# First rows re-laid in a graph-network kernel: norms ahead of unit rows, masks ahead of conversions

## The reference

```python
h = jnp.maximum(_layernorm(x, axis=-1), 0.0)
x = x + _L0_gnn_ref(h, adj, L0_gnn_beta)   # cosine attention, masked by adj
h = jnp.maximum(_layernorm(x, axis=-1), 0.0)
x = x + _L1_gnn_ref(h, adj, W_self, W_neigh)  # h @ W_self + (adj @ h / deg) @ W_neigh
# _L0_gnn_ref:
norm2 = jnp.linalg.norm(x, axis=1, keepdims=True)
cos = beta[0] * (x @ x.T) / (norm2 @ norm2.T + 1e-07)
P = jax.nn.softmax(cos + (1.0 - adj) * -1000000000.0, axis=1)
return P @ x
```

## Time and profile before

| | |
|---|---|
| three runs | 503.0 us median (502.96 to 504.5) |
| profiled execution | 502.87 us, span 500.9 us |
| busy share of the span | TensorE 94%, GpSimd 59%, ScalarE 60%, VectorE 56% |
| chain of waits | TensorE 87%, VectorE 5%, GpSimd 3%, DMA 2%, ScalarE 2% |

### The profile page before, as it was taken

How to read it: one execution, slowest core, us unless ns; L and a number is a source line. 1 busy time by engine, 2 the same in 40 slices (tenths; PEclk the granted TensorE clock), 3 DMA queues, 4 the chain that set the end, 5 groups by cost and what they waited for, 6 DMA issues and landing times.

```text
span 500.9 us, 12746 instructions
## 1 busy us (share of the span) xinstructions
PE 471.2 (94%) x5392; PEld 397.7 (79%) x5392; DVE 279.8 (56%) x686; ACT 298.1 (60%) x427; POOL 297.0 (59%) x261
## 2 busy tenths in 40 slices
PE   0768999999999999999999999999799999999996
PEld 0636788888788888888888888877688888888895
DVE  6975666567566585656765856757632321322153
ACT  2979787866986759876798598688730201110121
POOL 3889887877897768986799688888750000000000
PEclk9989999999999999999999999999999999999999
DMA  8057865655776557754676476563010000000001
GB/s 248 12 183 282 273 204 175 224 178 183 252 249 221 181 161 249 245 217 157 225 244 236 167 227 223 205 196 107 3 34 1 22 22 22 1 22 22 22 1 43
DMA packets 31549, 74.39 MB, mean 149 GB/s; under 512 B 2560, under 2 KB 15104, under 8 KB 31488
## 3 DMA queue, kind: packets, MB, share of 16 engines
q1 hardware_dynamic: 31488, 73.54, 43.8%
HBM read 71.43 MB, written 2.10 MB: 147 GB/s over the span
## 4 chain that ended last, share of the span: by engine, by line
PE 87%; DVE 5%; POOL 3%; DMA 2%; ACT 2%; issue 1%; SPq 0%; POOLq 0%; DVEq 0%; ACTq 0%
PE ps L1078 23%; PE ps L941 17%; PE ps L952 9%; PE ps L1005 6%; PE ps L1002 6%; PE ps L1004 6%; PE ps L979 5%; PE ps L982 5%; PE ps L981 5%; PE ps L1063 2%; PE ps L1052 2%; DVE adj_t L665 1%; DVE adj_t L644 1%; DMA stage<-in_adj_dram 1%; DMA x_sb<-in_x_dram 1%
## 5 line engine op out<-in xcount | busy, mean ns | idle before, releaser
L407 POOL TENSOR_TENSOR near<-word,adj_t 128x1024 f32<-128x1024 f32 x72 | 145.2, 2016 | 57.4 <-DVE word L778 56.4
L561 ACT ACTIVATE word<-ps,small 128x512 f16<-128x512 f32 x144 | 135.6, 942 | 70.8 <-PE ps L941 67.0
L778 DVE TENSOR_TENSOR word<-ps,word 128x512 f16<-128x512 f32 x144 | 106.3, 739 | 105.4 <-ACT ps L562 105.3
L1078 PE MATMUL ps<-table,adj_t 128*128 128x257 f16 x1024 | 116.8, 274 | 0.0
L941 PE MATMUL ps<-unit_t 128*128 128x512 f16 x432 | 106.7, 381 | 4.7 <-DVE word L778 4.7
L1078 PEld LDWEIGHTS ps<-table,adj_t 128*128 128x128 fp8e4 x1024 | 99.3, 98 | 13.0
L562 ACT ACTIVATE ps<-ps,small 128x512 f32<-128x512 f32 x144 | 107.2, 744 | 0.0
L1002 PE MATMUL ps<-table,near 128*128 128x129 f16 x576 | 102.6, 219 | 4.0 <-POOL near L407 2.6
L1005 PE MATMUL ps<-table,near 128*128 128x129 f16 x576 | 102.8, 222 | 0.0
L1004 PE MATMUL ps<-table,near 128*128 128x128 f16 x576 | 102.6, 219 | 0.0
L979 PE MATMUL ps<-table,far 128*128 128x129 f16 x448 | 79.9, 219 | 0.3
(11 more groups left out here) (94 smaller groups left out, 490.6 us busy)
## 6 DMA issues: line engine op xcount, KB each, us to landing
stage<-in_adj_dram SPq DMA_DIRECT2D x128, 512.0 KB, 4.4
x_sb<-in_x_dram SPq DMA_DIRECT2D x4, 512.0 KB, 6.2
x_again<-in_x_dram SPq DMA_DIRECT2D x8, 256.0 KB, 5.6
out_dram<-x_sb SPq DMA_DIRECT2D x7, 256.0 KB, 2.3
out_dram<-x_sb SPq DMA_DIRECT2D x1, 192.0 KB, 2.0
stage<-in_L_gnn_W_neigh_dram SPq DMA_DIRECT2D x1, 64.0 KB, 2.6
stage<-in_L_gnn_W_self_dram SPq DMA_DIRECT2D x1, 64.0 KB, 2.5
out_dram<-x_sb SPq DMA_DIRECT2D x1, 64.0 KB, 1.7
```

What stands on the lines that cost most here:

```text
L407: pool.tensor_tensor(ring(near, k), ring(word, k), adj_t[:, near_adj(k)], ALU.mult).then_inc(s_near, 1)
L561: act.activation(half(word16, k, c, 0, HIGH, TPS), score(k, c), ACT.Exp, bias=exp_bias, scale=exp_scale)
L778: dve.tensor_tensor(half(word16, k, c, 0, LOW, TPS), score(k, c), half(word16, k, c, 0, HIGH, TPS), ALU.subtract).then_inc(s_elo, 1)
L1078: return pe.matmul(ps[:, agg_bank(g) + t, 0:TW], adj_t[:, at:at + P], tab(b), start=(b == 0), stop=(b == T - 1))
```

## The change

The head's order is rewritten, and with it the first iterations of the middle. VectorE takes all four parts' statistics before the first norms, and all norms before its unit rows. The scale by HS = 256 is folded into small operations on GpSimd ahead of its powers; two small VectorE operations per part go. GpSimd takes all four powers of the variances ahead of the first norm power; its conversions of pair 2 stand behind mask 0. ScalarE does table_high(0) and units(3) behind its h tiles. The low half of the table of block 0 goes to VectorE. units(4) to units(6) go into VectorE's iterations 1, 3 and 5, units(7) into GpSimd's 6 and 7. TensorE sums all h tiles before the first scores; its order up to iteration 1 changes, and the first three transposes use other PSUM banks. SyncE loads two near and two far tiles at once. ScalarE converts its far tiles one pair later.

The diff, cut to its core:

```diff
-    RING = [("unit", 0), ("unit", 1), ("score", 0, 0), ("score", 0, 1), ("score", 1, 0), ("score", 1, 1), ("unit", 2)]
+    RING = [("score", 0, 0), ("score", 0, 1), ("score", 1, 0), ("score", 1, 1)]
...
-    LEAD = 3
+    CONVERT_AFTER = [[2], [3], [4], [5], [6, 7]] + [[k + 3] if k + 3 < NP else [] for k in range(5, NP)]
...
-            return 5 + AT["unit", g] % 3
+            return (3, 4, 2)[g] if g < 3 else 5 + AT["unit", g] % 3
...
+            load_near(0)
+            load_near(1)
+            load_far(FAR[0])
+            load_far(FAR[1])
+            for k in range(2, NP):
+                sp.wait_ge(s_adjd, k - 1)
+                load_near(k)
+                m = FAR_BEFORE[k]
+                if PAIR[k][2] and m >= 2:
+                    sp.wait_ge(far_sem(m), m // 2)
+                    load_far(k)
...
-                                   ).then_inc(s_rnorm_s, 1)
+                pool.tensor_scalar(var_e[:, part], mv_v[:, part, 1], HS ** -2, EPS * HS ** -2, ALU.mult, ALU.add
+                                   ).then_inc(s_scaled_e, 1)
+                pool.wait_ge(s_scaled_e, i + 1)
+                pool.tensor_tensor(scale_h[:, part], var_e[:, part], neg_half, ALU.pow).then_inc(s_rstd, 1)
+
+            def inverse_norms(first, last):
+
+                part = slice(first * TX, (last + 1) * TX)
+                pool.wait_ge(s_norm2, last + 1)
+                pool.tensor_scalar(norm2_g[:, part], norm2[:, part], HS ** -2, 1e-20 * HS ** -2, ALU.mult, ALU.max
+                                   ).then_inc(s_scaled_n, 1)
+                pool.wait_ge(s_scaled_n, min(last, 2) + 1)
+                for i in range(first, last + 1):
+                    part = slice(i * TX, (i + 1) * TX)
+                    pool.tensor_tensor(rnorm[:, part], norm2_g[:, part], neg_half, ALU.pow).then_inc(s_rnorm, 1)
...
-                for t in range(g * TPS, (g + 1) * TPS):
-                    pool.tensor_scalar(u_rows(t, t + 1), h_rows(t, t + 1), rnorm[:, t:t + 1], HS, ALU.mult, ALU.mult
-                                       ).then_inc(s_unit_p, 1)
+                for t in range(g * TPS + a, g * TPS + b):
+                    pool.tensor_scalar(u_rows(t, t + 1), h_rows(t, t + 1), rnorm[:, t:t + 1], None, ALU.mult).then_inc(s_unit_p, 1)
...
-            inverse_norm(0)
+            inverse_std(3)
+            inverse_norms(0, 0)
             units(0)
-            inverse_std(3)
-            inverse_norm(1)
-            scaled_inverse_norm(1)
             convert(0)
-            inverse_norm(2)
+            inverse_norms(1, 1)
...
-            inverse_norm(3)
-            units(7)
+            inverse_norms(2, 3)
             convert(1)
-            convert(2)
-            convert_far(2)
...
-                if s == 0 and k % 2 == 0:
-                    low_parts(k // 2)
-                if k + LEAD < NP:
-                    convert(k + LEAD)
-                    if PAIR[k + LEAD][2] and FAR_BEFORE[k + LEAD] % 2 == 0:
-                        convert_far(k + LEAD)
+                if s == 0 and k % 2 == 1 and (k + 1) // 2 < NS:
+                    low_parts((k + 1) // 2)
+                for ahead in CONVERT_AFTER[k]:
+                    convert(ahead)
+                    if PAIR[ahead][2] and FAR_BEFORE[ahead] % 2 == 0:
+                        convert_far(ahead)
+                if k in (6, 7):
+                    units(7, 2 * (k - 6), 2 * (k - 6) + 2)
...
+            for i in range(XP - 1):
+                first_h(i, i * TX, (i + 1) * TX)
+            first_h(XP - 1, T - TX, T - TX + 4)
+            unit_high(0)
+            first_h(XP - 1, T - TX + 4, T)
+            act.wait_ge(s_h, TPS)
+            table_high(0)
+            units(3)
...
+                    if k <= 1:
+                        unit_high(k + 1)
                     if k % 2 == 0 and 3 <= k // 2 + 1 < NS:
                         unit_high(k // 2 + 1)
-                    if k == 0 or k % 2 == 1 and (k + 1) // 2 < NS:
+                    if k % 2 == 1 and (k + 1) // 2 < NS:
                         table_high((k + 1) // 2)
-                    if k + 2 < NP and PAIR[k + 2][2] and FAR_BEFORE[k + 2] % 2 == 1:
-                        convert(k + 2)
+                    if k + 1 < NP and PAIR[k + 1][2] and FAR_BEFORE[k + 1] % 2 == 1:
+                        convert(k + 1)
...
                 then(last)
+
+            def variances(i):
+
                 for t in range(i * TX, (i + 1) * TX):
                     last = dve.bn_aggr(mv[:, t * 2:(t + 1) * 2], stats[:, t * 6:(t + 1) * 6])
-                then(last)
-                dve.tensor_scalar(var_e[:, i * TX:(i + 1) * TX], mv_v[:, i * TX:(i + 1) * TX, 1], EPS, None,
-                                  ALU.add).then_inc(s_var, 1)
+                last.then_inc(s_var, 1)
...
                 part = slice(i * TX, (i + 1) * TX)
+                dve.wait_ge(s_var, i + 1)
                 dve.wait_ge(s_rstd, i + 1)
-                then(dve.tensor_scalar(scale_h[:, part], rstd[:, part], HS, None, ALU.mult))
                 dve.scalar_tensor_tensor(bias_h[:, part], mv_v[:, part, 0], -1.0, scale_h[:, part],
...
-                then(last)
-                dve.tensor_scalar(norm2_g[:, part], norm2[:, part], 1e-20, None, ALU.max).then_inc(s_norm2, 1)
+                last.then_inc(s_norm2, 1)
...
-                    dve.tensor_scalar(u_rows(t, t + 1), h_rows(t, t + 1), rnorm[:, t:t + 1], HS,
-                                      ALU.mult, ALU.mult).then_inc(s_unit, 1)
+                    dve.tensor_scalar(u_rows(t, t + 1), h_rows(t, t + 1), rnorm[:, t:t + 1], None, ALU.mult).then_inc(s_unit, 1)
+
+            def first_low_parts():
+
+                dve.wait_ge(s_hh, 1)
+                dve.tensor_tensor(tab_v[:, 0:TPS, 0:D], by_tile(h_rows(0, TPS)), tab_v[:, 0:TPS, D:2 * D], ALU.subtract
+                                  ).then_inc(s_tab_first, 1)
 
...
+            row_sums(0)
             variances(0)
+            row_sums(1)
             variances(1)
             scales(0)
+            row_sums(2)
             variances(2)
             scales(1)
+            row_sums(3)
+            variances(3)
+            scales(2)
             norms(0)
-            scales(2)
-            variances(3)
+            scales(3)
             norms(1)
-            scales(3)
             norms(2)
-            units(1)
-            unit_low(0)
             norms(3)
+            dve.wait_ge(s_norm2, XP)
             then(dve.tensor_reduce(out=least, in_=norm2, axis=mybir.AxisListType.X, op=ALU.min))
             dve.tensor_scalar(least, least, -1.0, None, ALU.mult).then_inc(s_least, 1)
-            unit_low(1)
-            units(2)
+            unit_low(0)
+            units(1)
+            dve.wait_ge(s_hsum, 1)
+            dve.tensor_scalar(no_edge[:, 0:D], ps[:, 1, 0:D], TINY, None, ALU.mult).then_inc(s_mean, 1)
+            first_low_parts()
             dve.wait_ge(s_flag, 1)
             any_small = dve.value_load(small_norm[0:1, :], min_val=0, max_val=1)
-            units(4)
-            units(5)
-            units(6)
-            dve.wait_ge(s_hsum, 1)
-            dve.tensor_scalar(no_edge[:, 0:D], ps[:, 1, 0:D], TINY, None, ALU.mult).then_inc(s_mean, 1)
+            units(2)
...
-                unit_low(2)
+                    unit_low(k + 1)
...
+                    if k in (1, 3, 5):
+                        units(4 + k // 2)
...
-            sum_of_h(TX, T - TX)
+            sum_of_h(TX, T)
+            scores(0)
+            for i in range(3):
+                score_product(1, 0, i)
             unit_transpose(1)
-            scores(0)
-            sum_of_h(T - TX, T)
-            scores(1)
+            for i in range(3):
+                score_product(1, 1, i)
             unit_transpose(2)
+            for i in range(3):
+                score_product(2, 0, i)
             pe.wait_ge(s_first, 5)
             pe.wait_ge(s_mean, 1)
             for k in range(NP):
+                if k == 0:
+                    attend_near(0)
+                    for i in range(3):
+                        score_product(2, 1, i)
+                    continue
...
```

More of the change, by code:

```diff
@@ L88, in gnn_program @@
         mv = early(7, T * 2)
-        var_e, rstd, scale_h, bias_h, norm2, norm2_g, rnorm, rnorm_s = [early(7, T) for _ in range(8)]
+        var_e, scale_h, bias_h, norm2, norm2_g, rnorm = [early(7, T) for _ in range(6)]
+        mv_v = mv.rearrange("p (t c) -> p t c", c=2)
         ones_w = early(6, P)
@@ L263, in gnn_program @@
         s_rnorm = sem("rnorm_ready")
-        s_rnorm_s = sem("rnorm_scaled")
+        s_scaled_e = sem("variance_scaled")
+        s_scaled_n = sem("norm2_scaled")
         s_unit_p = sem("unit_by_gpsimd")
@@ L271, in gnn_program @@
         s_hh = sem("table_high_ready")
+        s_tab_first = sem("first_table_ready")
         s_tab = sem("table_ready")
@@ L321, in load_x_again, with load_near, load_far @@
```

(45 more changed lines are left out.)

5 lines of the change are left out of this document (1 added, 4 removed).

## The result

The changed kernel takes 509.9 us (median of 4 runs, 509.46 to 510.28) beside 502.99 for the one before: ratio 1.013, 95% interval 1.0109 to 1.015. The profiled execution has a span of 507.9 us, 7.0 more than 500.9.

A forecast was written before the change was run, and what follows sets the result against it. TensorE was taken to bound the middle, so only the start of units(3)'s transposes counts: 2.2 us earlier (0.6 from the first exponential, 1.6 from the removed stall), 502.87 - 2.2 = 500.7 us; range over cases 499.4 to 503.1, without the exclusion.

The forecast's parts named there:

- slower rival: VectorE's unit rows in iterations 1, 3, 5 wait for whole GpSimd operations: 3.2 to 12.8 us lost, 503.9 to 513.5; chance 0.10.
- the sums stay slow: Head: TensorE's sums of h keep the pace of 7 per us; first exponential 30.6, time 503.1, no change; chance 0.12.
- 0.95 stays: nothing lost: Iterations 1, 3, 5: four unit rows (0.86 us) fit VectorE's 1.81 us idle; without cover up to 2.6 in all.
- the visits: The four unit rows of units(4), units(5) or units(6) in VectorE's iteration 1, 3 or 5, forecast at about 0.86 us each.
- The rule: Skill text: double-pace VectorE tensor_scalar and GpSimd operations exclude each other; unit rows' 278 ns was taken to speak against it.
- The rival's price: Exclusion in iterations 1, 3, 5: one wait 2.0 us, four 5.2, less 0.95 spare, times three: 3.2 to 12.8.
- Head, units(0): GpSimd's first four unit rows, behind all variance powers and the first norm power: 1.59 us long, ending at 21.0.
- Head, the sums: TensorE's 48 passes over 24 h tiles before the first scores: from 22.15 to 27.4, the pace rising at 25.1.
- From the first exponential to the transposes: Pairs 0 to 3: from 28.2 to the transposes of units(3) at 43.9 instead of 46.08; removed stall gains 1.6.
- Slack of GpSimd and of the far loads: Middle: units(7) makes GpSimd 1.0 late once, far loads queue up to 1.1 ahead; both costed zero, bounds 0 and 1.0.

The follow-up runs named there:

- before_moved: The kernel before with only units(4) to units(6) moved from VectorE's head into its iterations 1, 3 and 5, old two-factor form; 509.29 us, ratio 1.011.
- one_op: The changed kernel with one two-input VectorE operation of 512 elements in place of four of 128 in iterations 1, 3 and 5; ratio 0.999 to the kernel before.
- on_scalar: The changed kernel with units(4) to units(6) on ScalarE, two tiles behind the exponentials of pairs 4 to 9; 504.1 us beside 504.42 for the kernel before.
- both_mended: The changed kernel with units(4) to units(6) on ScalarE and 28 of 32 h tiles summed ahead of the first transposes; 501.34 us beside 504.27 before.
- pool_form: both_mended with GpSimd's unit rows in their old form (second factor 1.0); ratio 0.9902 to the kernel before.

## Why the prediction was wrong

It named the mechanism as its slower rival, gave it 0.10, and forecast 500.7; the measured 509.9 lies inside that rival's 503.9 to 513.5. The head came out as a second rival had it, that the sums stay slow (0.12): first exponential 30.6 there and 30.85 here, and "no change" at the transposes, which start at 46.10. Step by step:

- **"0.95 stays: nothing lost", the visits (the step that failed).** The prediction charged 0.86 a visit, hidden in 1.81 of idle time. Measured: 5.08, 4.38, 4.37. The reading behind it was that 278 ns in the median and 323 at most over 20 operations mean that a unit row does not wait for GpSimd. But in the trace of before these 20 ran beside GpSimd's powers on 8 elements and its 128-element unit rows, never beside a mask or a conversion of 1024. A power is long enough to wait for, and they did not wait for it:

```profile
27.91 1.69 POOL L386 TENSOR_TENSOR adj_t<-adj_t,small 128x8 f32<-128x8 f32 x1
28.88 0.87 DVE L675 TENSOR_SCALAR adj_t<-adj_t 128x128 f32<-128x128 f32 x4 [0.24 <-issue]
```

  So it is the kind of the GpSimd operation that counts, and not its length alone; what sets the power apart (its eight elements a lane, or its kind of work) no run shows. The maximum of 323 was itself a wait: the three unit rows of 314 to 323 ended 0.07 to 0.08 behind one of GpSimd's, and GpSimd's took 0.43 to 0.60 each beside them (29.70, 1.87 for the four) where they take 0.37 in before_moved with VectorE's out of the way. And the 0.28 each of the per-partition operations at 360.92, beside a mask, was read as clearing a per-partition scalar; those operations read PSUM as their first input. What they and the unit rows share, the scalar, was the wrong thing to compare. VectorE's wait at 22.69, beside a conversion, was the row that spoke for this case: the same operation (L669) took 0.17 at 20.14, beside a power.
- **The rule.** The Trainium skill ("SBUF — State Buffer", "SBUF: two separate sides") says a VectorE operation in a two-port mode, or one with two SBUF inputs against a GpSimd operation that reads SBUF, and the GpSimd operation lock each other out for a whole instruction. The runs agree for masks, low parts and conversions: each of the four operations of the first visit ends where a GpSimd one does, and one_op, with two SBUF inputs, waits too. They do not agree for the powers, which read SBUF as well and held up no unit row (above); there the measurement decides. By the Trainium skill ("VectorE: DVE Perf Modes") fp32 tensor_scalar would also run at twice the pace; the least duration here is 262 to 273 ns, hardly under the 0.28 each of the operations at 360.92 that read PSUM and a second tensor. I took the missing gain in pace as proof of the missing lock. It is none.
- **The rival's price.** It said 5.2 a visit when all four wait, less 0.95 of spare time: 12.8 in all. The waits beyond 0.86 were 4.2, 3.5 and 3.5; less 0.95 each, 8.4 are left. TensorE idled 5.0 of them, in four waits for VectorE's low parts behind 46.5 us, and the lower clock behind the first hole, which no rival had, makes about 1.6 more. That the rest was hidden by TensorE's work on the running pair is argued, not tested.
- **Head, units(0).** Forecast to end at 21.0, they ended at 22.3: 2.88 us instead of 1.59. The form that was costed at nothing cost 0.24 an operation, the norms beside them the rest.
- **Head, the sums.** Forecast 5.25 us, measured 6.69. The counts of 7 and 12 passes in a window of 1 us were read as a rate. Matmuls overlap in the record and are counted in every window that they touch; 48 in 6.69 us are 7.2 in a microsecond, in a trace whose windows say 6 to 12. Counted by their starts they are 5 in a microsecond and then 9. That the pace would rise was right, and nearly when (forecast 25.1, measured about 26); both rates were too high. Together with units(0) this is the 2.65 between the 28.2 forecast and the 30.85 measured, within 0.1.
- **From the first exponential to the transposes.** Forecast 15.7 us, measured 15.25, against 17.28 before: the stall on the first far tile is gone, as reckoned. This gain of 2.0 was the only one, and the later first exponential (2.05) took it whole. That the transposes start where they did before is two sizes cancelling, not a head that did not change.
- **Slack of GpSimd and of the far loads.** Held: in on_scalar TensorE is busy all of the 50 us from 50 to 100.

## What to carry to other kernels

In this kernel VectorE's tensor_scalar from SBUF to SBUF and its operation with two SBUF inputs waited for GpSimd's masks, low parts and conversions to end, once per operation. Its low parts and far masks, with an input in PSUM, did not, nor did two other operations that read SBUF alone (last section). Before moving small VectorE work into a stage where GpSimd is busy with long operations on large tiles, count operations, not elements, and give it to ScalarE or make it one operation. An undisturbed duration says nothing of waiting unless the rows show what ran beside it, of the kind that it will meet. And take a rate from the start of the first to the end of the last instruction, not from counts in short windows.

## What the runs showed of the hardware

- The two engines take turns. When GpSimd's operation ended, VectorE's waiting unit row ran (0.2 us), and the following one again waited for the next GpSimd operation to end: three times running behind the first wait in the first visit, and twice behind the first wait in each of the others.
- Reading SBUF alone does not make a VectorE operation wait. The row statistics of the rows that the middle finishes (x in SBUF, 128 x 128) and a reciprocal ran beside masks of the changed kernel at their own pace: 0.87 for four from 129.53, beside the mask of 129.73 to 131.75, and at most 0.295 each over all 32; 0.18 each for all eight reciprocals, seven of them inside a mask.

```profile
129.53 0.87 DVE L774 BATCH_NORM_STATS2 small<-x_sb 128x6 f32<-128x128 f32 x4
129.73 2.02 POOL L419 TENSOR_TENSOR near<-word,adj_t 128x1024 f32<-128x1024 f32 x1 [1.93 <-DVE word L802]
```

- On GpSimd, a tensor_scalar of 128 x 128 fp32 with a per-partition factor alone took 0.67 us in the median, with a second factor of 1.0 it took 0.43 (0.60 and 0.37 at the least). The form with one factor fewer is the slower one.
- TensorE waits 2.6 us for GpSimd's mask at the last block in every kernel here, before too. In both_mended the granted clock fell behind it, in pool_form not (start:end, length, TensorE busy, clock, DMA share, GB/s):

```profile
358.00:360.00 2.00, 0.73 (x11) 0.94 0.01 4
360.00:362.00 2.00, 2.00 (x19) 0.50 0.56 165
```

```profile
356.00:358.00 2.00, 0.51 (x9) 1.00 0.01 4
358.00:360.00 2.00, 2.00 (x30) 1.00 0.51 145
```

  At 0.50 (1.2 GHz) the same matmuls take longer; both_mended had a mean clock of 0.990, pool_form 1.000. Times of one and the same kernel lie in two groups 1.6 us apart (the kernel before beside on_scalar: six of 19 at 502.74 to 502.96, all at 0.993, eleven at 504.4 to 504.7, mostly at 0.987), so that a part of a difference of two medians can be this: of the 3.4 us between the two spans of both_mended and pool_form, 1.8 are the head's. No experiment set that clock apart.
